# The spike drive is copied out of its PSUM bank by ACT, and the bank goes back at once

## The chip, the cores and the metric
The kernel runs on one core of a Trainium2 chip. The metric is the device time of one execution in microseconds. An engine named PE is TensorE, DVE is VectorE, ACT is ScalarE, POOL is GpSimd and SP is SyncE.

## The reference
Two transformer layers run over 8 sequences of 512 tokens by 256 channels. Each has a layer norm ahead of every block, and a residual. The change is in the second block of the first layer, a feed-forward whose output goes through five steps of a spiking neuron:

```
h = square(relu(x @ W_fc.T))           # 256 -> 1024
y = h @ W_proj.T                       # 1024 -> 256, "the drive"
def step(mem, _):
    reset = (mem - 1 > 0)
    mem_new = 0.9 * mem + y - reset
    return mem_new, (mem_new - 1 > 0)
out = (sum of the 5 spikes) / 5;   x = x + out
```

The drive y is constant over the five steps, so the number of spikes of a value is the number of five fixed thresholds that y reaches. The kernel counts them in five compare passes over y.

## The kernel before
Every sequence passes through layer 0's attention (pass (0, s), 96 score units) and layer 1's attention (pass (1, s), 40 score units). The passes alternate: (0, 0), (0, 1), (1, 0), (0, 2), (1, 1) and so on, ending with (0, 7), (1, 6), (1, 7). The feed-forward of a sequence is laid between the steps of a pass by tables of due times (`MID_A`, `MID_B`, `MID_C`): that of sequences 0 to 6 runs in passes (0, 1) to (0, 7), that of sequence 7 in pass (1, 6). All steps of a pass are sorted by due time into one list, and PE, DVE, ACT, POOL and SP each walk the same list and issue their own part of each step, in that order.

PSUM has 8 banks of 128 x 512 values. Three (`outs`) hold attention outputs. The other five (`work`) are a ring: `plan_banks` walks the step list and gives each use of a bank the next number, cyclically. PE may fill a bank again only when the readers of its former use are done. A bank can be held (`hold`): the ring then skips it, so that four banks rotate, until it is discarded from `held`.

A feed-forward is done in two halves of 256 tokens. For half i of sequence n:
- `hT`: PE transposes the normalised rows, ACT copies them to `HT[:, :, 256 i : 256 i + 256]` (`half_out`, recorded at L1742).
- four steps `fc`: PE multiplies by `WFC` (L1262), ACT applies Relu (L1872), POOL squares (L2016).
- four steps `y` (0 to 3): PE multiplies by `WFP` (L1273, 8 matmuls a step) into one held bank, which the plan holds from step `y` 0.
- six steps `spike` on DVE. Pass 0 (L1663) compares the bank with the first threshold and writes the residual buffer `X2` (or `WKW` in the last sequence), called total. Passes 1 to 4 (L1665) compare the bank with a threshold and add total. Pass 5 (L1672) scales total by 0.2 and adds `X1`. Each waits for the one before. The bank is discarded from `held` at pass 4.
- `var`, `ln`, and the transposes and projections (`qk`) of the next block.

Between `y` 3 and `spike` 0 lie 8 score units in the first half of sequences 0 to 6, 4 in their second half, and 1 in sequence 7. Between them run the steps of layer 0's attention: `max` (PE L1147, DVE L1461 and L1464: row maxima of the scores), `mt` (PE L1155, or L1161 in layer 1: their transposes), `unit` (PE L1181 to L1183, or L1185 in layer 1; ACT exponentials L1857), `mask` (POOL L1972), `pv` (PE L1218, or L1237 in layer 1), and `piece` and `piece_tr`, which prepare the next pair of heads. A `piece` of kind qk is PE L1085 and L1089, then DVE L1423 (rotation products `AB`), then POOL L1961 (sum to `TOK`) and ACT L1742 (`TOK`, `VV`). Piece 6 is PE L1100. `piece_tr` is PE L1112, then ACT L1742 (high part to `BIG`), then DVE L1442 (low part). L1413 is piece 2's low part. DVE also scales attention outputs (L1484), and POOL adds them (L1988, L1990).

Of the kernel before, what the change touches and what calls it, by code (L numbers as in the profile page):

```python
# [14 lines left out]
ALU = mybir.AluOpType  # L15
# [433 lines left out]
def plan_banks():  # L449
    work = Banks(NWORK)  # L450

    def piece(g, m, what):
        work.use((what, g, m), {"nope": 4, "val": 2}.get(PIECES[m][0], 3) if what == "piece" else 2)

    def prologue(n, j):
        for name in (["hT0", "hT1"], ["small0", "small1"], ["score_cols", "gate"], ["nqT", "ckvT"],
                     ["pos"], ["selT"], ["imp"])[j]:
            work.use(("pro", n, name))

    def attention(layer, s):  # L460
        for x in STEPS[layer, s]:
            what, n = x[0:2]
            if what in ("unit", "max", "mt"):
                work.use((s, layer) + x, {"unit": 0, "mt": 2}.get(what, 1))
            elif what in ("next_max", "next_mt"):
                work.use((x[-1], 1, what[5:]) + x[1:-1], {"next_mt": 2}.get(what, 1))
            elif what in ("piece", "piece_tr"):
                piece(n, x[2], what)
            elif what == "kr":
                work.use(x, 2)  # L470
            elif what == "pro_pe":
                prologue(n, x[2])
            elif what in ("hT", "fc", "v", "sign"):
                work.use(x)
            elif what in ("proj_early", "wo_early"):
                for i in range(2):
                    work.hold((what.split("_")[0], n, i))
            elif what == "proj_add":
                work.held.discard(work.of["proj", n, x[2]][0])
            elif what == "tail_add":  # L480
                work.held.discard(work.of["wo", n, x[2]][0])
            elif what == "y" and x[3] == 0:
                work.hold(("y", n, x[2]))
            elif what == "spike" and x[3] == 4:
                work.held.discard(work.of["y", n, x[2]][0])
            elif what == "qk":
                work.use(x, 2)
            elif what == "heads":
                for k in range(2):
                    work.use(x + (k,), 2 - k)  # L490

    attention(*BEGIN)
    for z in PASSES:
        attention(*z)
    for x in TAIL_ORDER:
        if x[0] == "wo_early":
            for i in range(2):
                work.hold(("wo", B - 1, i))
        elif x[0] == "tail_add":
            work.held.discard(work.of["wo", B - 1, x[1]][0])  # L500
        elif x[0] in ("hT", "sign"):
            work.use((x[0], B - 1) + x[1:])
    return work
# [58 lines left out]
def build_program(nc, x, w_small, w_imp, w_q, w_nv, w_kw, w_sel, w_proj, g_q, g_kv,  # L562
                  w_fc, w_ffp, w_qkv, w_o, w_sign,
                  rope0, cos1, sin1, ident, causal, before, earlier, ranks, out):
    work = plan_banks()
    ctx = ExitStack()
    with ctx:
# [31 lines left out]
        X1, X2 = sb("X1", [P, NT, C]), sb("X2", [P, NT, C])  # L599
        HN = sb("HN", [P, NT, C])  # L600
        HN0 = sb("HN0", [P, NT, C])
        HT = sb("HT", [P, NC, T])
# [44 lines left out]
        WB = [ctx.enter_context(nc.psum_tensor(f"work{k}", [P, 512], F32)) for k in range(NWORK)]  # L647
# [4 lines left out]
        def sem(name):  # L652
            return ctx.enter_context(nc.semaphore(name))
# [3 lines left out]
        work_read = [sem(f"work_read{k}") for k in range(NWORK)]  # L657
# [37 lines left out]
        spiked = sem("spiked")  # L695
# [6 lines left out]
        def full(e, use, bank):  # L702

            ring, sems, banks = bank
            k, _, f, _, _ = ring.of[use]
            e.wait_ge(sems[k], f)
            return banks[k]

        WORK = (work, work_full, WB)
# [23 lines left out]
        def x2(n):  # L733
            return X2 if n < B - 1 else WKW[:, :, :, :].rearrange("p n c k -> p (n c) k")
# [34 lines left out]
        def was_read(e, ring, sems, use):  # L769

            k, _, _, r, _ = ring.of[use]
            e.wait_ge(sems[k], r)
# [46 lines left out]
        THRESHOLDS = spike_thresholds()  # L819
# [537 lines left out]
        def _(dve):  # L1357
            v = nc.vector
            count = [0]

            def then(ins):

                count[0] += 1
                ins.then_inc(dve_step, 1)
                dve.wait_ge(dve_step, count[0])

            def read_work(ins, use):
                ins.then_inc(work_read[work.of[use][0]], 1)
# [285 lines left out]
            def spikes(n, i, k):  # L1654


                use, half = ("y", n, i), slice(2 * i, 2 * i + 2)
                total = x2(n)[:, half, :].rearrange("p t c -> p (t c)")
                if k == 0:
                    ps = full(dve, use, WORK)  # L1660
                    if i == 0 and 0 < n < B - 1:
                        dve.wait_ge(x_stored, 16 * n)
                    then(v.tensor_scalar(total, ps[:, :], THRESHOLDS[0], None, ALU.is_ge))  # L1663
                elif k < 5:
                    ins = v.scalar_tensor_tensor(total, WB[work.of[use][0]][:, :], THRESHOLDS[k], total, ALU.is_ge, ALU.add)  # L1665
                    if k < 4:
                        then(ins)
                    else:
                        read_work(ins, use)
                        was_read(dve, work, work_read, use)  # L1670
                else:
                    v.scalar_tensor_tensor(total, total, 0.2, X1[:, half, :].rearrange("p t c -> p (t c)"), ALU.mult,  # L1672
                                           ALU.add).then_inc(spiked, 1)

            def rope(n, t):
                use = ("qk", n, t)
# [61 lines left out]
        def _(act):  # L1738
            a = nc.scalar

            def copy(dst, src):
                return a.activation(dst, src, ACT.Copy)  # L1742

            def read_work(ins, use):
                ins.then_inc(work_read[work.of[use][0]], 1)
# [120 lines left out]
            def relu(n, i, f2):  # L1866
                use = ("fc", n, i, f2)
                ps = full(act, use, WORK)
                f = NF // 2 * i + f2
                if f >= 2:  # L1870
                    act.wait_ge(squared, NF * n + f - 1)
                read_work(a.activation(HIDDEN[:, f % 2, :], ps[:, :], ACT.Relu), use)  # L1872

            def stack_high(n, t, half):
                act.wait_ge(roped1, NT * n + t + 1)
                if half == 0 and t < 2:
                    act.wait_ge(stack_cleared, 2 * n + t + 1)
                else:

                    earlier = NT * half + t - 2  # L1880
                    full(act, ("heads", n, earlier % NT, earlier // NT, 1), WORK)
                h = H // 2
                q, k = (ROPED1[:, t, o + h * half:o + h * (half + 1), :].unsqueeze(2).broadcast_to([P, h, 2, D1])
                        for o in (0, H))
                copy(STACKS[t % 2][0][:, :, 0:4:3, :].bitcast(F32R), q).then_inc(stacked_hi, 1)
                copy(STACKS[t % 2][1][:, :, 0:2, :].bitcast(F32R), k).then_inc(stacked_hi, 1)
# [7 lines left out]
            def attention(layer, s):  # L1894
                for x in STEPS[layer, s]:
                    if x[0] == "piece":
                        piece(x[1], x[2])
                    elif x[0] == "piece_tr":
                        high_parts(x[1], x[2])
                    elif x[0] == "kr":  # L1900
                        high_rotated(x)
                    elif x[0] == "mt_out":
                        maxima_out(s, layer, x[1])
                    elif x[0] == "next_mt_out":
                        maxima_out(x[2], 1, x[1])
                    elif x[0] == "unit":
                        exponentials(s, layer, x[1], x[2])
                    elif x[0] == "out":
                        outputs(s, layer, x[1], x[2])
                    elif x[0] == "pro_act":  # L1910
                        prologue(x[1], x[2])
                    elif x[0] == "hT":
                        half_out(x, x[3], OT[:, 0:NC, :] if x[2] == 3 else HT)
                    elif x[0] == "fc":
                        relu(*x[1:])
                    elif x[0] == "v":
                        values_out(x[1], x[2])
                    elif x[0] == "stack":
                        stack_high(*x[1:])
                    elif x[0] == "heads":  # L1920
                        queries_out(*x[1:])
                    elif x[0] == "rows":
                        if s:

                            full(act, (s - 2, 1, "unit", NPAIR - 1, NU[1] - 1), WORK)
                        selecting_rows(x[1])
# [202 lines left out]
```

## Time and profile before

| what | value |
| --- | --- |
| median of 3 runs | 3028.03 us (3027.3 to 3029.63) |
| profiled execution, its own time | 3020.58 us |
| its span | 3018.4 us |
| granted TensorE clock, mean | 0.984 |
| PE busy | 2846.3 us, 94% |
| DVE busy | 1953.6 us, 65% |
| ACT busy | 1503.8 us, 50% |
| POOL busy | 961.6 us, 32% |
| spike passes 1 to 4 (L1665) | 64 instructions |

Busy time is the sum over the instructions of an engine, as a share of the span. An engine at 94% with short gaps sets the pace, and another's load counts only where PE waits for it. The profiled execution took 2.2 us more than its span.

### The profile page before, as it was taken

Reading aid. Unit: us, or ns where it says so; the run is one execution under the profiler, and the core shown is the slowest. Engines: PE = TensorE matmul, PEld = TensorE weight load, DVE = VectorE, ACT = ScalarE, POOL = GpSimd, SP = SyncE. Lnnn points to the kernel's source line nnn. Section 1 sums busy time; section 2 is a strip of 40 time slices with the busy share of each in tenths; the row PEclk is TensorE's granted clock in tenths of the full one; section 3 lists DMA queues with packets and bytes.
Section 4 is the critical chain, followed back from the end, with each engine's and each line's share of the span. In section 5 each row is a group of like instructions: output and inputs, shape, how many; then the busy total and the mean of one; then the engine's idle time right before and its main releaser. Section 6 shows DMA issues by size and latency. Waiting matters only on the chain. (4 is left out here: it accounts for less than half of the span.)

```text
span 3018.4 us, 53728 instructions
## 1 busy us (share of the span) xinstructions
PE 2846.3 (94%) x18384; PEld 2030.1 (67%) x18384; DVE 1953.6 (65%) x6243; ACT 1503.8 (50%) x3228; POOL 961.6 (32%) x1764
## 2 busy tenths in 40 slices
PE   6999899999999999999999999999999999999977
PEld 4666676667766677666776667766677666776654
DVE  5666656775677656866567766667566776665644
ACT  2554344564445644465444664446544464445543
POOL 1233233432334313333133332334222332233332
PEclk7999999999999999999999999999999999999999
DMA  3110001000110011100101001110011000110000
GB/s 124 34 33 27 26 26 40 25 18 19 47 33 25 25 32 32 33 20 25 38 26 33 25 19 38 34 38 12 30 35 38 26 16 26 33 33 18 14 8 29
DMA packets 58701, 91.44 MB, mean 30 GB/s; under 512 B 19904, under 2 KB 32704, under 8 KB 58176
## 3 DMA queue, kind: packets, MB, share of 16 engines
q1 hardware_dynamic: 58432, 88.01, 9.9%
q8 instruction: 149, 2.44, 0.3%
q14 instruction: 120, 0.98, 0.1%
HBM read 81.68 MB, written 5.24 MB: 29 GB/s over the span
## 5 line engine op out<-in xcount | busy, mean ns | idle before, releaser
L1857 ACT ACTIVATE PR<-work 128x512 f32<-128x512 f32 (+1 forms) x1088 | 642.0, 598 | 710.4 <-PE work L1183 610.3
L1461 DVE CUSTOM_DVE_ANT_0 work<-work,KEEPB 128x128 f32<-128x128 f32 (+3 forms) x1536 | 667.3, 476 | 93.0 <-PE work L1147 92.3
L1972 POOL TENSOR_SCALAR_AFFINE_SELECT PR<-PR 128x256 f32<-128x256 f32 (+1 forms) x960 | 350.2, 370 | 724.5 <-ACT PR L1857 719.1
L1147 PE MATMUL work<-BIG 96*128 96x448 f32 (+8 forms) x1664 | 445.7, 356 | 25.2 <-DVE NMX L1461 10.8
L1181 PE MATMUL work<-BIG 99*128 99x512 f32 (+4 forms) x1152 | 423.8, 368 | 17.5 <-DVE BIG L1442 6.1
L1961 POOL TENSOR_TENSOR TOK<-AB 128x256 f32<-128x256 f32 (+1 forms) x320 | 219.0, 686 | 597.9 <-DVE AB L1423 544.3
L1218 PE MATMUL outs<-PR,ONES 128*32 128x512 f32 (+4 forms) x2304 | 404.8, 458 | 0.0
L1182 PE MATMUL work<-BIG 96*128 96x512 f32 (+4 forms) x1152 | 382.6, 332 | 0.0
L1183 PE MATMUL work<-BIG 96*128 96x512 f32 (+4 forms) x1152 | 380.9, 331 | 0.0
L1442 DVE TENSOR_TENSOR BIG<-work,BIG 96x512 fp32r<-96x512 f32 (+1 forms) x320 | 192.1, 603 | 289.0 <-ACT BIG L1742 288.7
L1147 PEld LDWEIGHTS work<-BIG 96*128 96x128 f32 (+1 forms) x1664 | 267.0, 192 | 157.5 <-issue 80.4
L1742 ACT ACTIVATE BIG<-work 96x512 fp32r<-96x512 f32 (+4 forms) x592 | 334.4, 568 | 37.1 <-PE work L1112 28.0
L1742 ACT ACTIVATE TOK<-work 128x128 f32<-128x128 f32 (+1 forms) x320 | 85.4, 267 | 523.3 <-issue 241.3
L1218 PE MATMUL outs<-PR,VV 128*32 128x512 f32 (+3 forms) x2048 | 337.7, 440 | 3.2 <-POOL PR L1972 3.2
L1181 PEld LDWEIGHTS work<-BIG 99*128 99x128 f32 (+1 forms) x1152 | 210.3, 183 | 168.9 <-issue 107.6
L1089 PE MATMUL work<-WKW,HT 128*128 128x256 f32 x1024 | 273.3, 390 | 0.0
L1423 DVE TENSOR_TENSOR AB<-work,ROPE 128x512 f32<-128x512 f32 (+1 forms) x320 | 201.4, 630 | 85.4 <-PE work L1089 75.8
L1464 DVE TENSOR_REDUCE NMX<-work 128x1 f32<-128x64 f32 (+1 forms) x640 | 170.2, 282 | 123.5 <-PE work L1147 121.0
L1183 PEld LDWEIGHTS work<-BIG 96*128 96x128 f32 (+1 forms) x1152 | 213.2, 185 | 23.7
L1182 PEld LDWEIGHTS work<-BIG 96*128 96x128 f32 (+1 forms) x1152 | 212.6, 185 | 9.7 <-issue 3.4
L1089 PEld LDWEIGHTS work<-WKW,HT 128*128 128x128 f32 x1024 | 193.9, 196 | 15.7
L1112 PE MATMUL work<-ID,TOK 128*96 128x128 f32 x1152 | 180.5, 275 | 19.0 <-ACT VV L1742 8.2
(185 smaller groups left out, 4641.9 us busy)
## 6 DMA issues: line engine op xcount, KB each, us to landing
NRM<-park SPq DMA_DIRECT2D x112, 192.0 KB, 3.1
WKW<-w_kw_dram SPq DMA_DIRECT2D x64, 256.0 KB, 2.7
WSEL<-w_sel_dram SPq DMA_DIRECT2D x64, 256.0 KB, 2.9
R<-park SPq DMA_DIRECT2D x72, 64.0 KB, 2.0
HN<-x_dram SPq DMA_DIRECT2D x8, 512.0 KB, 4.8
X<-x_dram SPq DMA_DIRECT2D x8, 512.0 KB, 4.0
out_dram<-X SPq DMA_DIRECT2D x7, 512.0 KB, 3.2
R<-park SPq DMA_DIRECT2D x16, 192.0 KB, 3.0
```

Of the source, the lines that this page charges most:

```text
L1089: last = mm(ps[:, 192:448], HT0[:, c, t * P:(t + 1) * P], WKW[:, g % 2, c, :], start=(c == 0), stop=(c == NC - 1))
L1147: last = mm(ps[:, col:col + n], q, k, start=(i_mm == 0), stop=(i_mm == len(u["mm"]) - 1))
L1181: mm(out, k[0][0:D0 + 3], q[0][0:D0 + 3], start=(col == 0), stop=False)
L1182: mm(out, k[0][0:D0], q[1][0:D0], start=False, stop=False)
L1183: last = mm(out, k[1][0:D0], q[0][0:D0], start=False, stop=stop)
L1218: last = mm(OB[a][row:row + 32, j * P:T], v, PR[0:rows, slot, col:col + T - j * P], start=(j == 0), stop=(j == 2 or a == A2), skip_group_c ...
L1423: read_work(v.tensor_tensor(rotations(i, rows, heads), src.unsqueeze(1).broadcast_to(shape), ROPE0[0:rows, t, :, :].unsqueeze(2).broadcast ...
L1461: last = v.tensor_tensor_reduce(ps[:, lo:hi], ps[:, lo:hi], KEEPB[:, T - (hi - lo):T], -1.0, -NEG, ALU.add, ALU.min, dst)
L1742: return a.activation(dst, src, ACT.Copy)
L1857: a.activation(PR[0:rows, j % NP, :], ps[0:rows, :], ACT.Exp).then_inc(exp_ready, 1)
L1961: gp.tensor_tensor(dst.rearrange("p h (j d) -> p h j d", j=2), a4, b4[:, :, ::-1, :], ALU.add).then_inc(tok_ready, 1)
L1972: gp.affine_select(blocks, blocks, [[0, len(cols)], [1, P]], ALU.is_ge, 0.0, base=0, channel_multiplier=-1).then_inc(exp_masked, 1)
```

## The change
ACT gets a new step at `y` 3: it waits for the bank and copies it to `HT[:, :, 256 i : 256 i + 256]`, where the transposed rows of this half lay, which PE has read by then. That copy is now the bank's reader, and the plan discards the bank from `held` at `y` 3. The five threshold passes read the copy in SBUF, and pass 0 waits for ACT's copy in place of PE's products. Their views become 3-dimensional, [128, 2, 256]. Pass 5 computes as before.

```
-            elif what == "spike" and x[3] == 4:
+            elif what == "y" and x[3] == 3:
                 work.held.discard(work.of["y", n, x[2]][0])
...
-                use, half = ("y", n, i), slice(2 * i, 2 * i + 2)
-                total = x2(n)[:, half, :].rearrange("p t c -> p (t c)")
+                half = slice(2 * i, 2 * i + 2)
+                drive = HT[:, :, 256 * i:256 * (i + 1)]
+                total = x2(n)[:, half, :]
                 if k == 0:
-                    ps = full(dve, use, WORK)
+                    was_read(dve, work, work_read, ("y", n, i))
                     if i == 0 and 0 < n < B - 1:
                         dve.wait_ge(x_stored, 16 * n)
-                    then(v.tensor_scalar(total, ps[:, :], THRESHOLDS[0], None, ALU.is_ge))
+                    then(v.tensor_scalar(total, drive, THRESHOLDS[0], None, ALU.is_ge))
                 elif k < 5:
-                    ins = v.scalar_tensor_tensor(total, WB[work.of[use][0]][:, :], THRESHOLDS[k], total, ALU.is_ge, ALU.add)
-                    if k < 4:
-                        then(ins)
-                    else:
-                        read_work(ins, use)
-                        was_read(dve, work, work_read, use)
+                    then(v.scalar_tensor_tensor(total, drive, THRESHOLDS[k], total, ALU.is_ge, ALU.add))
                 else:
-                    v.scalar_tensor_tensor(total, total, 0.2, X1[:, half, :].rearrange("p t c -> p (t c)"), ALU.mult,
-                                           ALU.add).then_inc(spiked, 1)
+                    v.scalar_tensor_tensor(total, total, 0.2, X1[:, half, :], ALU.mult, ALU.add).then_inc(spiked, 1)
...
+            def drive_out(n, i):
+                use = ("y", n, i)
+                ps = full(act, use, WORK)
+                read_work(copy(HT[:, :, 256 * i:256 * (i + 1)], ps[:, :].rearrange("p (t c) -> p t c", t=2)), use)
...
+                    elif x[0] == "y" and x[3] == 3:
+                        drive_out(x[1], x[2])
```

## Rows read from the trace of the kernel before

**Rows 1.** The page, part 1: busy us, share of the span, instructions.
```profile
PE 2846.3 (94%) x18384; PEld 2030.1 (67%) x18384; DVE 1953.6 (65%) x6243; ACT 1503.8 (50%) x3228; POOL 961.6 (32%) x1764
```
**Rows 2.** Windows, from last `y` matmul to end of spike pass 4; busy us per engine.
```profile
1119.40:1147.60 28.20, 27.69 (x182) 20.09 (x181) 18.71 (x60) 8.72 (x20) 5.99 (x12) 1.00 0.25 72
1203.40:1220.10 16.70, 15.88 (x109) 10.73 (x107) 15.02 (x53) 5.42 (x13) 5.78 (x9) 1.00 0.02 5
2858.80:2865.10 6.30, 3.50 (x19) 2.85 (x18) 5.89 (x16) 2.26 (x4) 1.81 (x3) 1.00 0.13 34
sum 322.40, PE 305.30 PEld 214.18 DVE 237.67 ACT 112.18 POOL 85.25; mean PE 19.08 PEld 13.39 DVE 14.85 ACT 7.01 POOL 5.33
```
**Rows 3.** Waits of PE, whole span: total us, times, longest us.
```profile
PE work L1085 <- DVE X L1665: 5.4, 6, 0.9
PE work L1147 <- DVE WKW L1665: 2.8, 1, 2.8
PE work L1155 <- ACT VV L1742: 2.5, 6, 0.7
PE work L1147 <- DVE X L1665: 2.3, 2, 1.5
PE work L1185 <- DVE WKW L1665: 2.0, 1, 2.0
```
**Rows 4.** DVE instructions on tile X: ns min/median/max, first and last start us.
```profile
L1665 DVE SCALAR_TENSOR_TENSOR X<-work,X x56: 620/681/692, 423.6 to 2684.1; 128x512 f32<-128x512 f32 x56
L1663 DVE TENSOR_SCALAR X<-work x14: 673/677/681, 422.7 to 2677.9; 128x512 f32<-128x512 f32 x14
L1672 DVE SCALAR_TENSOR_TENSOR X<-X x14: 686/691/1445, 429.0 to 2684.9; 128x512 f32<-128x512 f32 x14
```
**Rows 5.** DVE instructions on tile WQKV.
```profile
L1497 DVE TENSOR_SCALAR WQKV<-WQKV x1: 419/419/419, 29.3 to 29.3; 128x512 f32<-128x512 f32 x1
```
**Rows 6.** ACT instructions on tile HT.
```profile
L1742 ACT ACTIVATE HT<-work x48: 585/597/613, 10.9 to 2895.2; 128x512 f32<-128x512 f32 x48
```
**Rows 7.** Timeline of DVE at spike pass 5, sequence 2, first half.
```profile
1148.21 1.44 DVE L1672 SCALAR_TENSOR_TENSOR X<-X 128x512 f32<-128x512 f32 x1
```
**Rows 8.** Timeline of POOL at the same time.
```profile
1148.07 1.03 POOL L2016 TENSOR_TENSOR R<-HN 128x512 f32<-128x512 f32 x1
1149.07 1.17 POOL L1961 TENSOR_TENSOR TOK<-AB 128x256 f32<-128x256 f32 x1
```
**Rows 9.** Timeline of DVE, sequence 2, second half.
```profile
1216.14 0.67 DVE L1665 SCALAR_TENSOR_TENSOR X<-work,X 128x512 f32<-128x512 f32 x1
1217.41 0.69 DVE L1423 TENSOR_TENSOR AB<-work,ROPE 128x512 f32<-128x512 f32 x1 [0.59 <-DVE X L1665]
1218.02 2.13 DVE L1665 SCALAR_TENSOR_TENSOR X<-work,X 128x512 f32<-128x512 f32 x3
...
1225.36 0.69 DVE L1442 TENSOR_TENSOR BIG<-work,BIG 96x512 fp32r<-96x512 f32 x1 [1.05 <-ACT BIG L1742]
```
**Rows 10.** Timeline of POOL, sequence 2, second half.
```profile
1215.76 1.27 POOL L1990 TENSOR_TENSOR OT<-NRM 64x512 f32<-64x512 f32 x1 [1.09 <-DVE NRM L1484]
...
1217.36 0.72 POOL L1961 TENSOR_TENSOR TOK<-AB 128x256 f32<-128x256 f32 x1
1218.24 0.73 POOL L1961 TENSOR_TENSOR TOK<-AB 128x256 f32<-128x256 f32 x1 [0.16 <-DVE AB L1423]
1218.92 0.41 POOL L1972 TENSOR_SCALAR_AFFINE_SELECT PR<-PR 128x256 f32<-128x256 f32 x1
```
**Rows 11.** Waits between 1225 and 1227 us.
```profile
PEld work L1100 <- DVE BIG L1442: 0.2, 1, 0.2
```
**Rows 12.** Timeline of ACT behind `y` 3, sequence 2, first half.
```profile
1120.17 0.60 ACT L1857 ACTIVATE PR<-work 128x512 f32<-128x512 f32 x1 [1.24 <-PE work L1183]
```
**Rows 13.** Timeline of PE, sequence 0, second half, 21 us behind spike pass 4.
```profile
521.12 0.50 PE L1181 MATMUL work<-BIG 99*128 99x512 f32 x1 [0.57 <-DVE BIG L1442]
```
**Rows 14.** Timeline of DVE, sequence 7, second half.
```profile
2885.89 0.69 DVE L1663 TENSOR_SCALAR WKW<-work 128x512 f32<-128x512 f32 x1 [2.56 <-PE work L1273]
```
**Rows 15.** Timeline of PE, sequence 7, second half, the next transposes.
```profile
2892.92 0.76 PE L959 MATMUL work<-ID,HN 128*128 128x128 f32 x4 [0.32 <-DVE HN L1393]
```

## The prediction
> **What bounds the kernel now.** I read the page's busy times first: PE is busy 94% of the span, DVE 65%, ACT 50% and POOL 32% [rows 1]. So PE sets the pace, and the change can gain only PE's gaps that hang on the held bank, and can lose only by making new ones. The windows view then takes the 16 stretches in which the bank is held but no longer filled, from the last `y` matmul to spike pass 4. They sum to 322.4 us, and PE is busy 305.3 of them [rows 2]: 17.1 us of gaps is all that five rotating banks could give. That is 0.57% of the time. PE's waits say what ended them [rows 3]: 12.5 us were released by spike pass 4 (5.4 + 2.8 + 2.3 + 2.0), because the next user got the held bank. Another 2.5 us are `mt` waiting for a bank that ACT reads. The rest are small. Last I read the timelines around single stretches, since a gap that goes is worth something only if the next release is not late as well.
>
> **Part 1, the DVE passes get another source.** Pass 0 reads SBUF in place of PSUM: 677 ns now [rows 4]; the row of the same shape with an immediate and both sides in SBUF took 419 ns [rows 5]. I take 419, 0.26 us less. Passes 1 to 4 take 681 ns now, with one input in PSUM [rows 4]. Pass 5 has both tensor inputs in SBUF: median 691, but up to 1445 ns [rows 4]. One of these long ones: DVE starts at 1148.21 and takes 1.44 us, and POOL's square had started at 1148.07 and ran to 1149.10; POOL's next instruction starts at 1149.07 and takes 1.17 us in place of the 0.72 that this sum takes elsewhere [rows 7, 8, 10]. So DVE stood until POOL was done, ran 0.55 us, and POOL stood for that. The PSUM passes show nothing of it: no L1665 is longer than 692 ns, though one at 1216.14 lies inside POOL's 1.27 us at 1215.76 [rows 4, 9, 10]. After the change 64 more passes have two inputs in SBUF. Each that meets POOL waits for POOL's instruction to end, and they take turns.
>
> The Trainium skill says this in "SBUF — State Buffer", section "Who interferes with whom": a VectorE instruction with two SBUF inputs contends with a GpSimd instruction that reads SBUF, and the loser is blocked for the whole instruction. The rows agree (1445 against 691 ns). The same skill, in "VectorE: DVE Perf Modes", errata section, gives VectorE a fixed cost of 58 cycles from SBUF against 120 from PSUM, by which 64 passes would each be 0.065 us shorter (estimate from that page); the rows do not show that (691 against 681 ns), so it is left out of the sum.
>
> **Part 2, where POOL is met on the path: second halves of sequences 1 to 6.** I work it out for sequence 2. Before: pass 1 at 1216.14, then 0.59 us of idle ahead of the rotation products, passes 2 to 4 from 1218.02 to 1220.15 [rows 9]. POOL in that time: 1.27 us from 1215.76, then 0.72, 0.73 and 0.41 [rows 10]. After: pass 1 waits until about 1216.9 and ends at 1217.4, 0.6 later, which the 0.59 of idle takes up. Pass 2 waits for the 0.72 sum until about 1218.5 and ends at 1219.1. Pass 3 waits for the 0.73 sum and ends at 1220.3; pass 4 waits for the 0.41 mask and ends at 1221.3. That is 1.1 us later than 1220.15. Everything behind it on DVE (pass 5, statistics, piece 2, the rotation products of piece 3) ran without a gap until ACT's `TOK` copy and the low part at 1225.36 [rows 9]. So DVE, not PE, is the chain here. Piece 6 on PE takes the bank that this low part frees, and it already waits for it: 0.2 us of its weight load [rows 11]. PE does get its 0.9 us at pass 4 [rows 3], runs 0.9 ahead, and gives them back at piece 6: the 5.4 us are worth nothing. The lateness of 1.1 us comes through almost whole: I take +1.05 each, +6.3 us for six. Bounds of each: -0.05 (no meeting) and +2.1 (also the 1.27 us instructions met with no idle to take them up, rows 10).
>
> **Part 3, first halves of sequences 1 to 6.** `mt` waits 2.5 us in all for a bank [rows 3], which the fifth bank saves. Spike pass 3 and 4 meet POOL there too, but pass 5's 1.44 us meeting [rows 7] gets shorter by as much, and DVE stands about 1 us for ACT behind it. I take -2.5 us together; bounds -4 (with the small gaps, rows 2) and +3.6 (0.6 us late in each, if a meeting reaches the path).
>
> **Part 4, sequence 0.** The waits for pass 4 are 2.3 us, 1.5 of them in the second half [rows 3]. In the second half DVE works on without a gap, and PE waits 0.57 us for DVE at 521.12 [rows 13], so only pass 0's 0.26 comes through. In the first half PE and DVE both stood, so the 0.8 comes through. I take -1.0; bounds -3 and +0.5.
>
> **Part 5, sequence 7.** PE waits 2.76 us for pass 4 in the first half [rows 3]; PE is busy only 3.50 of 6.30 us there [rows 2], and nothing else is late, as the next transpose of maxima needs only a reading done before. I take -2.7. In the second half DVE starts pass 0 the moment PE is done, at 2885.89 [rows 14], and the transposes at 2892.92 wait for DVE's rows [rows 15]. So PE's 2.0 us there are only moved, and the chain gets ACT's copy in it: 0.60 us [rows 6], less 0.26 for pass 0, plus about 0.9 for two or three masks of 0.41 us met on the way (the mask's length in rows 10): +1.2. Together -1.5; bounds -4.8 (all of rows 3's 2.8 and 2.0) and +1.2.
>
> **Part 6, what costs nothing.** ACT gets 16 copies of 0.60 us [rows 6]. Behind `y` 3 ACT stands idle for PE anyway, 1.24 us in sequence 2 [rows 12]; without that cover it would be 0.6 us for each exponential behind it. The copy waits for `y` 3; queued behind it on ACT are the exponentials of later units, which PE computes after `y` 3, so none waits for nothing. The plan gives the freed bank to the third or fourth use after `y` 3 (between `y` 0 and `y` 3 lie 9, 13 or 14 uses in sequences 0 to 6 and 5 and 2 in sequence 7, over four banks), when the copy is long done.
>
> **Sum.** +6.3 - 2.5 - 1.0 - 1.5 = +1.3 us. On the profiled execution: 3020.6 + 1.3 = 3021.9. It lies 7.45 us under the median of the runs shown; I add the same 1.3 to the median: 3029.3 us. A measurement here tells about 0.2%, 6 us, from no change.
>
> **The rivals.**
> - *The gaps come through and POOL is met rarely* (faster). For it: 12.5 us of waits name pass 4 as their releaser [rows 3]. Against: the wait at piece 6 [rows 11] and the 1445 ns [rows 4]. Without any meeting the sum is -0.3 - 3.0 - 1.0 - 2.4 = -6.7 (parts 2 to 5; I let part 3 gain 0.5 of its small gaps): 3021.3 us. The skill's advice in "VectorE: DVE Perf Modes", section "Rules for kernel authors", is to copy a matmul's result to SBUF first if many operations read it; that is this case. Chance 0.15.
> - *The shared access costs more than I let it* (slower). Its place is passes 1 to 4 of both halves. If part 2's meetings cost 1.7 each, and those of part 3 reach the path with 0.4 each in place of its gain, the sum is 10.2 + 2.4 - 1.0 - 1.5 = +10.1: 3038.1 us. It decides from 1.85 us a second half on with part 3 as forecast. For it: POOL itself is stopped as well, so masks and `TOK` come 0.5 us late. Against: such late masks are wanted microseconds later. Chance 0.2.
> - *The bank comes back no earlier*: ACT reaches its copy late, and PE waits for ACT where it waited for DVE. The gains go and +6.3 stays, plus 1.2 at the end: 3035.5 us. Against: the idle of rows 12. Chance 0.03, inside the slower ones.
>
> **How the numbers follow.** My case has 0.65 with a range of its own of 3024 to 3034. The range 3021 to 3036 takes in the faster rival's centre and half of the slower. Faster by over 6 us needs the first rival nearly whole: 0.14. Slower by over 6 us (past 3034.1): 0.22. Within: 0.64.
>
> **What would show it.** L1663 near 419 ns. L1665 with a median near 700 ns but many over 1000 in sequences 1 to 6, and POOL's L1961 longer where it follows one. No PE wait released by L1665. In second halves a PE gap of about 1.9 us before L1181 or L1100, released by ACT or DVE's L1442, in place of the 0.9. In sequence 7 no gap of 2.8, and a longer one ahead of the transposes. I am wrong if L1665 stays at 691 throughout, or if PE's gap at piece 6 stays under 0.5 us.

## The result, and the profile after

| | before | changed |
| --- | --- | --- |
| median, same chip and hour | 3027.66 us (3024.6 to 3029.63, 4 runs) | 3044.96 us (3043.29 to 3046.18, 4 runs) |
| ratio | | 1.0057, 95% interval 1.0045 to 1.0069 |
| profiled execution, its own time | 3020.58 us | 3043.29 us |

The change makes the kernel 0.57% slower: 17.3 us by the medians. The forecast, 3029.3 us with a range to 3036.0, was too low. The profiled executions differ by 22.7 us, because that of before lies 7 us under its median and that of after at the low end of its runs.

Busy times of the changed kernel, to be read against [rows 1]: DVE has 18 us more work and POOL 17, PE 9, ACT 9 (its 16 copies).

```profile
PE 2855.5 (94%) x18384; PEld 2034.1 (67%) x18384; DVE 1971.8 (65%) x6243; ACT 1513.2 (50%) x3244; POOL 978.7 (32%) x1764
```

The passes, as in [rows 4] (pass 0 is now L1664, passes 1 to 4 L1666, pass 5 L1668; columns: ns min/median/max, first and last start):

```profile
L1666 DVE SCALAR_TENSOR_TENSOR X<-HT,X x56: 620/775/3101, 424.1 to 2706.0; 128x512 f32<-128x512 f32 x56
L1664 DVE TENSOR_SCALAR X<-HT x14: 409/411/522, 423.3 to 2698.9; 128x512 f32<-128x512 f32 x14
L1668 DVE SCALAR_TENSOR_TENSOR X<-X x14: 681/686/693, 429.3 to 2706.8; 128x512 f32<-128x512 f32 x14
L1666 DVE SCALAR_TENSOR_TENSOR WKW<-HT,WKW x8: 686/734/1412, 2883.7 to 2909.0; 128x512 f32<-128x512 f32 x8
```

Pass 0 takes 411 ns as forecast. A pass of 1 to 4 takes 620 ns where it meets nobody, but the median is 775 and the longest 3101 ns, where [rows 4] had 692 at most. The place of the 3101 is pass 4 of the first half, in each of sequences 1 to 6. DVE and then POOL at that place in sequence 2 (start, duration):

```profile
1151.76 0.69 DVE L1423 TENSOR_TENSOR AB<-work,ROPE 128x512 f32<-128x512 f32 x1
1152.37 3.10 DVE L1666 SCALAR_TENSOR_TENSOR X<-HT,X 128x512 f32<-128x512 f32 x1
1155.51 0.69 DVE L1423 TENSOR_TENSOR AB<-work,ROPE 128x512 f32<-128x512 f32 x1
1156.11 0.68 DVE L1668 SCALAR_TENSOR_TENSOR X<-X 128x512 f32<-128x512 f32 x1
...
1159.83 1.40 DVE L1413 TENSOR_TENSOR BIG<-work,BIG 32x512 fp32r<-32x512 f32 x2 [1.77 <-ACT BIG L1737]
```
```profile
1151.27 1.59 POOL L1992 TENSOR_TENSOR OT<-NRM 64x512 f32<-64x512 f32 x1 [2.21 <-DVE NRM L1484]
1152.82 0.40 POOL L1974 TENSOR_SCALAR_AFFINE_SELECT PR<-PR 128x256 f32<-128x256 f32 x1
1153.19 0.73 POOL L1963 TENSOR_TENSOR TOK<-AB 128x256 f32<-128x256 f32 x1
1153.89 1.03 POOL L2018 TENSOR_TENSOR R<-HN 128x512 f32<-128x512 f32 x1
```

Pass 4 arrives in the last 0.5 us of POOL's addition. By part 1's rule it should have run when that ended, at 1152.86. It did not: the mask, the `TOK` sum and the square follow without a pause and at their full speed (0.40, 0.73, 1.03), and DVE ends at 1155.47, 0.55 us after the last of them. It stood through four POOL instructions, three of which began after it was there. The rotation products at 1155.51 are then 2.4 us later than they need be, and PE stands for what ACT makes of them, where before had no such gap (the timeline of PE, idle in brackets):

```profile
1156.82 0.61 PE L1112 MATMUL work<-ID,TOK 128*96 128x128 f32 x4 [0.87 <-ACT VV L1737]
1157.95 1.99 PE L1262 MATMUL work<-HT,WFC 128*128 128x256 f32 x8 [0.52 <-ACT BIG L1737]
```

In second halves they do take turns (DVE, then POOL, sequence 2):

```profile
1223.33 1.75 DVE L1666 SCALAR_TENSOR_TENSOR X<-HT,X 128x512 f32<-128x512 f32 x1
1225.12 0.69 DVE L1423 TENSOR_TENSOR AB<-work,ROPE 128x512 f32<-128x512 f32 x1
1225.73 2.82 DVE L1666 SCALAR_TENSOR_TENSOR X<-HT,X 128x512 f32<-128x512 f32 x3
...
1233.76 0.69 DVE L1442 TENSOR_TENSOR BIG<-work,BIG 96x512 fp32r<-96x512 f32 x1 [1.06 <-ACT BIG L1737]
```
```profile
1222.95 1.59 POOL L1992 TENSOR_TENSOR OT<-NRM 64x512 f32<-64x512 f32 x1 [0.76 <-DVE NRM L1484]
1224.50 0.85 POOL L1974 TENSOR_SCALAR_AFFINE_SELECT PR<-PR 128x256 f32<-128x256 f32 x1
1225.33 1.86 POOL L1963 TENSOR_TENSOR TOK<-AB 128x256 f32<-128x256 f32 x2
1227.15 0.86 POOL L1974 TENSOR_SCALAR_AFFINE_SELECT PR<-PR 128x256 f32<-128x256 f32 x1
```

Here the masks take 0.85 and 0.86 in place of 0.41: POOL is stopped too. From pass 1's start to pass 4's end it is 5.22 us (1223.33 to 1228.55) against 4.01 (1216.14 to 1220.15, [rows 9]).

PE's waits for L1665 [rows 3] are gone. The ones that grew (us in total, times, longest):

```profile
PE work L1112 <- ACT VV L1737: 12.4, 14, 3.7
PE work L1112 <- DVE BIG L1413: 8.3, 12, 0.9
PE work L1100 <- DVE BIG L1442: 6.1, 19, 0.6
```

They were 8.2 in 8, 3.6 in 7 and 4.0 in 12 before. What pass 4 no longer holds up, the later links of the same DVE chain now do.

PE runs the same 18,384 matmuls in the same order in both, so the k-th of one trace can be set against the k-th of the other, and the lag read stretch by stretch (each half from the last `y` matmul to 10 us behind pass 4's old place):

| stretch | forecast | profile | how |
| --- | --- | --- | --- |
| first halves, sequences 1 to 6 | -2.5 | +9.6 | each gains 1.0 to 1.6, then loses 2.7 to 3.1; +1.2 to +1.8 net |
| second halves, sequences 1 to 6 | +6.3 | +7.6 | each gains 1.8, loses 2.8; +1.0 net, one +2.6 |
| sequence 0 | -1.0 | +2.4 | first half -1.5, second +3.9 |
| sequence 7 | -1.5 | +0.1 | first half -2.6, second +2.7 |
| elsewhere | 0 | +3.0 | none over 1.2 |

### The profile page after: what moved, and what is told of

Read it like the earlier page. It is cut to its first block and busy times, and to the rows that moved or that the text cites. A ratio compares the mean times of both kernels' runs of the same rounds, so it can differ in the third digit from the quotient of the medians.

```text
span 3041.1 us, 53744 instructions
## 1 busy us (share of the span) xinstructions
PE 2855.5 (94%) x18384; PEld 2034.1 (67%) x18384; DVE 1971.8 (65%) x6243; ACT 1513.2 (50%) x3244; POOL 978.7 (32%) x1764
## 5 line engine op out<-in xcount | busy, mean ns | idle before, releaser
L1974 POOL TENSOR_SCALAR_AFFINE_SELECT PR<-PR 128x256 f32<-128x256 f32 (+1 forms) x960 | 359.7, 380 | 717.0 <-ACT PR L1852 709.7
```

The lines of the kernel that those rows point to most:

```text
L1974: gp.affine_select(blocks, blocks, [[0, len(cols)], [1, P]], ALU.is_ge, 0.0, base=0, channel_multiplier=-1).then_inc(exp_masked, 1)
```

## The experiments

Theory A: the loss is in DVE passes with two inputs in SBUF that meet POOL, above all in the six where POOL goes past them. Rival B: the loss comes from the plan, the clock or the copies (another bank order, ACT's work, the fifth bank), and the long passes are hidden. All ratios are to the kernel before on the same chip, with 95% intervals. The chips differ between the runs, so kernels are compared with one another by their ratios, 0.1% being 3 us.

**One SBUF input.** Passes 1 to 4 become a reduction of the copy alone. It leaves out thresholds 2 to 5.

```
-                    then(v.scalar_tensor_tensor(total, drive, THRESHOLDS[k], total, ALU.is_ge, ALU.add))
+                    then(v.tensor_reduce(SPARE[:, k:k + 1], drive, AX.XY, ALU.max))
```


> The changed kernel with passes 1 to 4 replaced by a maximum over the same 512 columns of the copy (one SBUF input instead of two; the comparisons with the second to fifth threshold are left out of the output). Theory A, shared access between DVE's two-input passes and POOL is the whole cost: no pass is longer than about 0.72 us, the 3.1 us passes and the +9.6 and +7.6 us of the first and second halves go, and the time is 3019 to 3024 us, 4 to 9 under the kernel before. Theory B, the copy on ACT or the other order of banks costs the time: it stays at 3038 to 3046.

Measured 3014.83 us, ratio 0.9964 (0.9951 to 0.9976): 10.9 us under the kernel before, where 4 to 9 was expected, and some 28 us under the changed kernel, with the same plan, copies and nearly the same instruction length:

```profile
L1667 DVE TENSOR_REDUCE SPARE<-HT x64: 619/676/687, 424.1 to 2881.6; 128x1 f32<-128x512 f32 x64
```

In sequence 2 this pass 4 starts at 1147.36 and takes 0.68 us beside the same run of POOL instructions, addition to square (1146.26 to 1149.59); the first instruction with two SBUF inputs behind it, pass 5, is the one that waits (1.47 us). First halves of sequences 1 to 6 gain 0.5 to 1.3 us each, second halves 0.6 to 0.7, where the changed kernel loses 1.6 and 1.0. The gap at the next pieces goes with the second SBUF input. The reduction also writes one column in place of 512, but the passes of before wrote 512 and none was longer than 692 ns [rows 4], so it is not the write that meets POOL. B falls as the main cause.

**POOL waits for its own second addition.** POOL's mask then starts a moment after the addition, not with it. It was so only for odd pairs of heads.

```
-                if p % 2:
-                    pool.wait_ge(summed, NPAIR * s + p + 1)
+                pool.wait_ge(summed, NPAIR * s + p + 1)
```


> The changed kernel, but POOL waits for the end of its own second addition (L1992) for every pair of heads, where it did so only for odd pairs. Theory A1, POOL keeps the access because its next instruction is already handed over when the addition ends: with the wait DVE gets its turn behind the addition, pass 4 in the first halves of sequences 1 to 6 takes about 1.0 us instead of 3.1, and the time falls by 7 to 12 us to 3033 to 3038. Theory A2, POOL goes first whenever both want the access: the pass stays at 3.1 us and the time within 3 us of 3045.

Measured 3031.50 us, ratio 1.002 (1.0011 to 1.0029): some 11 us better than the changed kernel, within the 7 to 12 expected. The same place of sequence 2:

```profile
1152.77 1.04 DVE L1666 SCALAR_TENSOR_TENSOR X<-HT,X 128x512 f32<-128x512 f32 x1
```
```profile
1151.67 1.59 POOL L1992 TENSOR_TENSOR OT<-NRM 64x512 f32<-64x512 f32 x1 [2.21 <-DVE NRM L1484]
1153.33 0.74 POOL L1974 TENSOR_SCALAR_AFFINE_SELECT PR<-PR 128x256 f32<-128x256 f32 x1
1154.05 0.72 POOL L1963 TENSOR_TENSOR TOK<-AB 128x256 f32<-128x256 f32 x1
```

Pass 4 arrives at the same point of the addition, ends 0.55 us after it, and the mask stands for it: 0.74 in place of 0.40. A gap of 0.07 us on POOL (the addition ends at 1153.26, the mask starts at 1153.33) goes with 1.04 us in place of 3.10. The first halves then give -0.2 to -0.8 each, -2.8 together, in place of +9.6.

**That wait by itself**, in the kernel before (same edit).

> The kernel before with one edit: POOL waits for its own second addition for every pair of heads, not for odd ones alone. No copy, no changed source. Theory A (the wait matters only by giving DVE passes with two SBUF inputs their turn; before has few of these): within 0.1% of before, ratio 1.000, and pass 5 at the 1445 ns meetings unchanged. Rival (the wait is itself a gain or a loss, so that the kernel with the waits was faster than the changed one for another reason): off by 0.15% or more, most likely faster by as much as the 13 us between those two kernels.

Measured 3025.4 us, ratio 1.0 (0.9991 to 1.0009). The wait has no measurable effect of its own, and pass 5 still meets POOL:

```profile
L1672 DVE SCALAR_TENSOR_TENSOR X<-X x14: 687/692/1571, 430.1 to 2688.2; 128x512 f32<-128x512 f32 x14
```

**The bank held as before** until pass 4, all else as changed.

```
-            elif what == "y" and x[3] == 3:
+            elif what == "spike" and x[3] == 4:
```


> The changed kernel, but the ring of banks skips the bank until spike pass 4, as before the change; ACT still copies and DVE still reads the copy. This takes away the fifth bank alone. If the fifth bank is worth what PE's small gaps in the held stretches suggest (2.5 us of mt's waits and some tenths), the time is 3046 to 3049 us. If the waits for pass 4 were all the gain, it is the same as the changed kernel, 3045 within 1.5.

Measured 3040.96 us, ratio 1.0048 (1.0035 to 1.006). I had expected a larger loss without the fifth bank, and it came out some 3 us under the changed kernel, with overlapping intervals: in the changed kernel the fifth bank is worth nothing that can be measured.

**ACT's copy alone.** The kernel before with the copy added; DVE waits for it and goes on reading PSUM.

```
+                    k0, _, _, r, _ = work.of[use]
+                    dve.wait_ge(work_read[k0], r - 1)
...
+                    elif x[0] == "y" and x[3] == 3:
+                        drive_out(x[1], x[2])
```


> The kernel before with ACT's copy added and nothing else: DVE reads PSUM, waits for the copy as well, and the bank is held until pass 4. If ACT's 16 copies cost nothing but at the end (0.6 us in sequence 7), the time is 3027.7 to 3029.5 us. If they cost time elsewhere (theory B), it is 3032 or more.

Measured 3026.14 us, ratio 1.0001 (0.9992 to 1.001): sixteen copies cost nothing that can be measured (-2.4 to +3.0 us), as part 6 said.

**The change in parts.** Four kernels apply all of it only where a condition holds, and are as before elsewhere (`def early(n, i): return ...`, asked where the bank is released, where ACT copies and where DVE picks its source).

First halves of sequences 1 to 6 (`i == 0 and 0 < n < 7`):

> The change in the first halves of sequences 1 to 6 alone; all other halves read PSUM and hold the bank as before. Comparing matmul by matmul, the changed kernel lost 9.6 us around these six halves. If the halves are independent: +9 to +10.5 us, 3037 to 3038. If the loss needs the other halves: under +5.

Measured ratio 1.0031 (1.0019 to 1.0042), +9.4 us. Its passes show it whole: only 24 read the copy, and the median hides the six.

```profile
L1681 DVE SCALAR_TENSOR_TENSOR X<-HT,X x24: 676/685/3106, 779.4 to 2624.2; 128x512 f32<-128x512 f32 x24
```

Second halves of sequences 1 to 6 (`i == 1 and 0 < n < 7`):

> The change in the second halves of sequences 1 to 6 alone. The prediction said +1.05 us each, +6.3; the changed kernel's trace shows +1.0 in five of them and 2.6 in sequence 3. Expected: +6 to +7.6 us, 3034 to 3035. If the rival of the prediction held (gaps come through, POOL rarely met): 3022 to 3027.

Measured 1.0025 (1.0016 to 1.0035), +7.6 us. Here all are moderately long:

```profile
L1681 DVE SCALAR_TENSOR_TENSOR X<-HT,X x24: 773/986/1761, 852.5 to 2695.6; 128x512 f32<-128x512 f32 x24
```

Second halves of sequences 0 and 7 (`(n, i) in ((0, 1), (7, 1))`):

> The change in the second halves of sequences 0 and 7 alone. In the changed kernel the first lost 3.3 us, with the granted TensorE clock at half for 10.2 us there, and the second +2.7 against a gain of 2.6 in the half before. If the short gaps behind the wait that goes bring the clock down: half clock near 503 us and +3 to +6 us in all. If the clock fell there by chance: 0 to +2 us.

Measured 0.9999 (0.999 to 1.0008), which is -0.3 us (-3.0 to +2.4). I had expected +3 to +6 us if the short gaps of PE bring the clock down, and 0 to +2 if it fell by chance, so the time does not bear out the first. The profile of this run has the half clock again (from 502.7, for 6.8 us). First halves of sequences 0 and 7 (`(n, i) in ((0, 0), (7, 0))`):

> The change in the first halves of sequences 0 and 7 alone, the two in which the changed kernel gained: 1.5 and 2.6 us. Expected 3022 to 3025 us, 3 to 5 under the kernel before, which would beat both. If the rest of sequence 7 waits for DVE whatever PE gains: -1.5, 3026.

Measured 0.9981 (0.9971 to 0.999), 5.7 us under the kernel before where 3 to 5 was expected: faster than either kernel. A second sample:

> The early copy in the first halves of sequences 0 and 7 alone, a second sample of the kernel that has already been timed so, beside the one with the copy in all first halves. Expected ratio 0.998 (0.997 to 0.999) again. If it comes out at 0.999 or above, part of the first sample's gain was in the placing of the runs.

Measured 0.9985 (0.9976 to 0.9994). The four parts add up to 9.4 + 7.6 - 0.3 - 5 = +11.7 us, each with about 3 us of uncertainty, against 17.3 (13.6 to 20.9) for the whole. The 5.6 us between them are within these uncertainties together, and whether the parts also act on one another was not shown.

**The version that the parts point to.** The early copy in all first halves, with POOL's wait; second halves as before (`i == 0`).

> The early copy in the first half of every sequence, the bank held and read by the passes as before in every second half, and POOL waits for its own second addition for every pair of heads. Theory A (DVE gets its turn at the shared reads once POOL does not issue without a pause, and the gains of first halves then come through): first halves of sequences 1 to 6 give about -0.4 us each as in the kernel with the waits, -2.4 together; the first halves of sequences 0 and 7 give what they gave alone, about -4.5 together; sum -7 us, ratio 0.9977 (0.996 to 0.999). Rival (the wait on POOL costs something of its own in the stages where nothing is copied, or the two gains do not add): ratio 0.999 to 1.001. It would be the fastest with copies in place.

Measured 3017.08 us, ratio 0.9975 (0.9966 to 0.9983): 7.6 us faster than before by the ratio, where -7 was expected, and some 25 faster than the change. Its passes: 28 read the copy, 1251 ns at most, and 28 read PSUM.

```profile
L1681 DVE SCALAR_TENSOR_TENSOR X<-HT,X x28: 621/685/1251, 423.6 to 2611.0; 128x512 f32<-128x512 f32 x28
L1681 DVE SCALAR_TENSOR_TENSOR X<-work,X x28: 622/683/693, 494.8 to 2683.4; 128x512 f32<-128x512 f32 x28
```

In its trace the first halves of sequences 1 to 6 give -0.3 to -0.9 each, -3.3 together, and those of sequences 0 and 7 -1.5 and -2.6, against the trace of before.

## Why the prediction was wrong

**Part 1 had the resource and missed its rule.** That two SBUF inputs meet POOL was right, and so was "waits for POOL's instruction to end". The step that failed is the half sentence behind it, "and they take turns". I had it from one meeting [rows 7, 8]. In the six first halves DVE waited for four POOL instructions. The kernels with POOL's wait, one SBUF input and first halves alone show that this made those halves slow: with the wait, or with one SBUF input, nothing is left of the +9.6.

The Trainium skill, "SBUF — State Buffer", section "Who interferes with whom", says that a VectorE instruction with at most one SBUF input, outside the modes that take both ports, does not contend with GpSimd; the reductions agree (687 ns at most, 64 of them). It also says that the order of issue decides who blocks and that the loser waits for the whole instruction. The six passes differ: they had been issued and were waiting when the mask began at 1152.82, and stood for 2.1 us more, through three instructions that began later.

**Part 2 was right in the meetings and the sum, not in the path to PE.** Forecast +1.05 a half, measured +1.0 in five of six. The sixth lost 1.6 more while the granted clock stood at 0.53, half of full speed, from 1605.0 to 1608.4. The kernel with these halves alone measured +7.6 us against the forecast 6.3. The waits on DVE were placed a little wrong (pass 1 waited longest, 1.75 us, and the addition that it met before ended at 1217.03, not at 1216.9), but their sum was close: 1.2 us where 1.1 was worked out. The way to PE was not the one forecast. I had put the whole loss, a gap of about 1.9 us, at piece 6 (L1100), and had named a gap there under 0.5 us as a sign of being wrong. It is 0.30 or 0.31 in all six. PE loses its time in four gaps, 2.02 us together in sequence 2:

```profile
1228.06 0.41 PE L1218 MATMUL outs<-PR,VV 128*32 128x256 f32 x2 [0.33 <-POOL PR L1974]
1232.12 0.61 PE L1112 MATMUL work<-ID,TOK 128*96 128x128 f32 x4 [0.90 <-DVE BIG L1413]
1233.22 0.50 PE L1181 MATMUL work<-BIG 99*128 99x512 f32 x1 [0.49 <-ACT VV L1737]
1234.50 1.13 PE L1100 MATMUL work<-WSEL,SELT 128*128 128x256 f32 x4 [0.30 <-DVE BIG L1442]
```

The first ends with a mask of POOL that came late, and the prediction had held against the second rival that such masks are wanted only microseconds later. Two of the others end with low parts of DVE, one with a copy of ACT. PE had run 1.8 us ahead, not 0.9, and gives back 2.8, so the net of 1.0 is DVE's lateness and came out although both its terms were too small.

**Part 3 is where the forecast was lost**: +9.6 in place of -2.5, and outside its bounds of -4 to +3.6. The upper bound let a meeting cost 0.6, one POOL instruction. With POOL's wait in place the same halves give -2.8, and -3.3 in the fastest version, near the -2.5 that the part forecast: the gain is there, its condition was not seen. That it comes from the fifth bank was not tested by itself.

**Part 4.** The first half gave -1.5, more than the 0.8 forecast. The second shows +3.9: it gains 1.6 and then loses 5.6, as the granted clock falls to half for 10 us behind pass 4 (columns: window, its us, busy us of PE, PEld, DVE, ACT, POOL with counts, granted clock, DMA share, GB/s).

```profile
502.50:512.70 10.20, 9.76 (x38) 6.37 (x41) 8.96 (x41) 1.79 (x3) 2.96 (x5) 0.51 0.13 46
```

The profiled execution of before has 1.00 there. But of the eight profiles in which this half is as before, five have a fall, and have lost 1.7 us (four of them) or 3.6; of the five in which it is changed all have one, with 1.7 to 3.9 us of net loss. So about 1.3 us of the 3.9 is the luck of one profile of before, and in the average of these few profiles the changed half is some 2 us dearer. In it PE stands for DVE's maxima twice before the fall at 502.7 (0.50 and 0.74 us) and again just behind it (0.44). All eight unchanged ones have one wait of 1.5 us there instead, and five fell and three did not: that the gaps bring the clock down is not shown. The forecast counted DVE's time alone and had no term for the clock.

**Part 5.** The first half gave -2.6 against a forecast of -2.7. In the second the chain grew by 0.55 us, not 1.2: ACT's copy costs 0.6 as worked out, but the masks only 0.08 each. Yet the half lost 2.7. PE now does early what it used to do late, so it stands 3.6 us in one piece before the transposes, and works on at half the clock. PE's timeline, then two windows, up to the transposes and behind them:

```profile
2908.45 1.07 PE L1237 MATMUL outs<-PR,NRM 128*32 128x384 f32 x16 [0.76 <-POOL PR L1974]
2913.11 1.09 PE L959 MATMUL work<-ID,HN 128*128 128x128 f32 x4 [3.59 <-DVE HN L1393]
```
```profile
2905.50:2912.50 7.00, 3.26 (x32) 1.42 (x31) 5.92 (x16) 2.66 (x5) 2.18 (x4) 1.00 0.13 37
2912.50:2920.00 7.50, 6.46 (x21) 3.14 (x22) 2.77 (x9) 1.79 (x3) 0.73 (x2) 0.54 0.00 1
```

The same two windows of the kernel before, where PE's 2.0 us gap lay earlier:

```profile
2885.90:2892.90 7.00, 4.68 (x32) 1.96 (x31) 6.59 (x17) 2.28 (x4) 2.15 (x5) 0.76 0.15 37
2892.90:2900.00 7.10, 6.31 (x26) 3.00 (x27) 3.47 (x10) 1.79 (x3) 1.13 (x2) 0.99 0.01 1
```

The clock was back (0.99) when the transposes came; now it is at 0.54, and the four take 1.09 us where they took 0.76 [rows 15]. Before, the clock was at half for 3.4 us from 2889.6, behind the 2.0 us gap; now it is for 6.8 us from 2912.5. I had called the moved gap free. The kernel with only the two second halves changed shows the same 3.59 us gap and transposes of 1.08 us. That the gap is what brings the clock down was not tested by itself, and other traces speak against so plain a link. With ACT's copy alone no gap is moved, and this half still lost 2.3 us, with the clock at half for 3.4 us from 2897.7. With the first halves of sequences 0 and 7 changed, and in the fastest version, PE has the same gaps there (2.02 and 1.65 us): the first kernel lost 1.6 us in both its profiles, at half clock for 3.4 us, and the fastest version lost nothing. Nor do the times show what these two second halves cost in the profiles: changed alone, they gave -0.3 us (-3.0 to +2.4), where the profiles read +2 and +2.7. What parts 4 and 5 lost to the clock stays open.

**The sum and the rivals.** Of the 22.7 us between the profiles, 12.1 over the forecast come from part 3, 1.3 from part 2, 3.4 from part 4, 1.6 from part 5, and 3.0 lie elsewhere. By the medians the change cost 17.3 us: the profile of before was a fast one, and some 5 us of these terms are that and not the change (the kernel with the wait alone, as fast as before by its times, ends 3.4 us behind that profile). The first rival fell with the meetings, which came in every half of sequences 1 to 6. The second rival had the sign and the resource, but not the form: it spread a small excess over all meetings, where all but six cost about what I had forecast, and those six cost 2.4 us each. Its 3038.1 us was 7 short. My range ended two us short even of that.

**What stays open**: why POOL goes past DVE at this one place. The traces of the changed kernel, of the one with the bank held and of the one with these first halves alone have 18 such arrivals, and POOL goes past in all 18 (by three later instructions in 17, by two in one). In every other meeting with POOL instructions that follow without a pause, in all the traces, DVE ended about 0.55 us after the first. The same addition and mask meet pass 1 in second halves, and there DVE gets its turn; that pass arrives 0.4 us after the addition's start, pass 4 of the first halves 1.1 us after it and 0.5 before its end. With POOL's wait an arrival just as late gets its turn, so the lateness alone does not do it.

## What to carry to other kernels

Before moving a VectorE operand from PSUM to SBUF, count the operation's SBUF inputs: from one to two makes it share reads with GpSimd, and a single meeting may cost the whole run of GpSimd instructions that follows without a pause. Judge such a change place by place on the chip: here twelve of its sixteen places cost 17 us and two gained 5, and one wait that changes nothing measurable by itself made some 11 of the 17 us go. A single profile can have luck with the granted clock: read a term of 1 to 2 us from several.

## What the runs showed of the hardware

- A DVE pass with two SBUF inputs takes 620 to 693 ns alone, as with one in PSUM. Where it meets a POOL instruction it ends about 0.55 us after that one. At one place it stood through four of them, 3.10 us, 17 times in three kernels.
- With a wait of POOL on its own previous instruction, which left a gap of 0.07 us, DVE got in behind the first (1.04 us in place of 3.10).
- A DVE reduction with one SBUF input ran beside the same POOL instructions with no loss (687 ns at most of 64).
- The granted TensorE clock fell to half for 6.8 or 10.2 us near 502 us in ten of the thirteen profiles. In the eight that have the same work and the same 1.5 us gap of PE there, it fell in five.
- It was at half for 6.8 us from 2912.5, at the end of 3.6 us of PE's idle time, where the kernel before had 3.4 us from 2889.6, behind a gap of 2.0 us.
